# Gated cross-attention and a routed FFN on one core: the reduction of a step's first maxima is moved ahead of a layer norm's aggregation, and a third of w2's load is moved ahead of four index loads

## The reference, cut to what matters

```
x   (32, 112, 256)   ctx (32, 375, 256)   16 heads of 16
Q = LN(x) @ Wq + bq;  K = ctx @ Wk + bk;  V = ctx @ Wv + bv
attn = softmax(Q K^T / sqrt(16)) per head
x = x + tanh(g_xattn) * ((attn V) @ Wo + bo)
xf = LN(x).reshape(3584, 256)
scores = softmax(xf @ w_router.T);  w, i = top_k(scores, 2)      # 8 experts
y_e = (silu(xf @ w1[e]) * (xf @ w3[e])) @ w2[e]                  # H = 352
x = x + tanh(g_ffn) * sum_k w_k * y_{i_k}
```

## Time and profile before

| | before |
|---|---|
| median of 3 runs | 848.33 us (844.21 to 849.57) |
| the profiled execution | 848.78 us, span 847.0 us |
| TensorE | 805.1 us busy (95%) |
| VectorE, ScalarE, GpSimd | 490.0, 436.1, 525.4 us busy |
| granted TensorE clock, mean | 0.989 |
| chain that ended last | PE 70%, DVE 11%, SP's queue 8%, DMA 4% |
| DMA | 112.33 MB, 133 GB/s mean |

### The profile page before, as it was taken

One profiled execution on the slowest core, in us unless ns is written; L12 is line 12 of the kernel. 1 busy time (PEld: TensorE's weight loads), 2 busy tenths in 40 slices (PEclk: granted clock), 3 DMA queues, 4 the chain that ended last, 5 costly groups with the idle time before them and its releaser, 6 DMA issues.

```text
span 847.0 us, 22216 instructions
## 1 busy us (share of the span) xinstructions
PE 805.1 (95%) x7529; PEld 696.9 (82%) x7529; DVE 490.0 (58%) x1170; ACT 436.1 (51%) x1120; POOL 525.4 (62%) x599
## 2 busy tenths in 40 slices
PE   7889999999999999999999999888999999999995
PEld 6679899998998999999999998756777777777773
DVE  5576777877877777787777777733622222222221
ACT  3356766766676676677666666554222222222221
POOL 6554555566576667657666765436677766666652
PEclk8899999999999999999999999999999999999998
DMA  6857867776676666676657565574344444443332
GB/s 159 209 142 175 200 171 191 191 191 169 168 183 162 153 160 154 160 183 149 149 135 172 135 162 136 149 195 78 52 63 64 73 66 64 63 63 64 63 58 30
DMA packets 99733, 112.33 MB, mean 133 GB/s; under 512 B 29164, under 2 KB 81012, under 8 KB 99624
## 3 DMA queue, kind: packets, MB, share of 16 engines
q1 hardware_dynamic: 79608, 92.48, 44.4%
q0 software_dynamic: 18512, 17.60, 13.4%
q10 hardware_dynamic: 1504, 0.85, 0.5%
HBM read 35.48 MB, written 17.53 MB: 63 GB/s over the span
## 4 chain that ended last, share of the span: by engine, by line
PE 70%; DVE 11%; SPq 8%; DMA 4%; issue 3%; POOL 1%; ACT 1%; ACTq 0%; POOLq 0%; DVEq 0%
PE ps L1473 17%; PE ps L1536 10%; PE ps L1212 8%; PE ps L1195 7%; PE ps L1226 6%; PE ps L1180 6%; DVE negmax L919 5%; PE ps L1219 3%; PE ps L1329 3%; PE ps L1388 2%; PE ps L1492 2%; SPq L285 2%; DMA w_sb<-in_L_ffn_w_dram 2%; SPq L286 2%; SPq L290 2%
## 5 line engine op out<-in xcount | busy, mean ns | idle before, releaser
L919 DVE TENSOR_REDUCE negmax<-ps 112x2 f32<-112x750 f32 x256 | 239.8, 938 | 111.1 <-PE ps L1212 102.9
L620 ACT ACTIVATE probs<-ps 125x448 f32<-125x448 f32 x384 | 208.9, 545 | 83.8 <-PE ps L1180 65.1
L399 POOL DMA_DIRECT2D stack<-negmax_t x128 | 68.3, 537 | 175.3 <-ACT negmax_t L675 164.2
L1180 PE MATMUL ps<-stack 97*125 97x224 f32 x768 | 163.7, 295 | 0.6 <-ACT probs L620 0.4
L1212 PE MATMUL ps<-stack 96*112 96x376 f32 x512 | 141.3, 357 | 14.2 <-DVE negmax L919 10.3
L523 POOL DMA_INDIRECT out_dram<-y,idx x63 | 100.8, 1600 | 69.4 <-issue 32.0
L1180 PEld LDWEIGHTS ps<-stack 97*125 97x125 f32 x768 | 126.2, 187 | 7.7 <-ACT probs L620 1.2
L719 ACT ACTIVATE silu<-ps 128x352 f32<-128x352 f32 x63 | 29.3, 465 | 188.2 <-PE ps L1473 161.9
L1131 DVE TENSOR_TENSOR h<-silu,ps 128x352 f32<-128x352 f32 x63 | 32.8, 520 | 143.9 <-PE ps L1473 138.9
L1536 PE MATMUL ps<-w_sb,h_t 128*128 x378 | 92.3, 380 | 3.1 <-DMA w_sb<-in_L_ffn_w_dram 2.4
L1212 PEld LDWEIGHTS ps<-stack 96*112 96x112 f32 x512 | 71.8, 178 | 23.7 <-DVE negmax L919 14.0
(11 more groups left out here) (239 smaller groups left out, 1500.5 us busy)
## 6 DMA issues: line engine op xcount, KB each, us to landing
stack<-split SPq DMA_DIRECT2D x252, 150.0 KB
stack<-split SPq DMA_DIRECT2D x127, 94.0 KB
ctx_raw<-in_ctx_dram SPq DMA_DIRECT2D x29, 375.0 KB, 3.9
stack<-split SPq DMA_DIRECT2D x127, 56.0 KB
out_dram<-xa SPq DMA_DIRECT2D x32, 112.0 KB, 2.4
xn_scratch<-xn SPq DMA_DIRECT2D x32, 112.0 KB
xa<-in_x_dram SPq DMA_DIRECT2D x7, 448.0 KB, 4.2
w_sb<-in_L_ffn_w_dram SPq DMA_DIRECT2D x16, 176.0 KB
```

Source lines behind the costliest of these rows:

```text
L399: gp.dma_start(dst[:, :, SKP + SQ * h:SKP + SQ * h + SQ], negmax_t[4 * h:4 * h + 4, half, :].bitcast(f32)).then_inc(s_nmrow[half][c % NSLO ...
L620: act.activation(probs[:, n % NP, :], ps[0:KW, EXPB + k % 2, 0:4 * SQ], ACT.Exp).then_inc(s_exp, 1)
L919: dve.tensor_reduce(negmax[:, half, :, p4], ps[0:SQ, m1:m2 + 1, 0:SK], axis=AX.X, op=ALU.max, negate=True).then_inc(s_max, 1)
L1180: last = pe.matmul(ps[0:KW, EXPB + k % 2, QW * m:QW * m + QW], stack[:, place_of(b), p, KW * ch:KW * ch + KW], stack[:, place_of(b), p, SK ...
```

## The change

Two edits. VectorE's reduction of the first pair of maxima of a step (t = 0, for batches 1 to 31; batch 0 keeps its place) is no longer taken in slot 0 behind `xn`, but in slot 11 of the step before. The copy of the logits moves up too, so that slot 11 now reads: copy of the logits, first maxima of batch i+2, aggregation, halving. In SyncE's list, the load of w2's first 128 rows (1024 KB) stands directly behind the eight loads of w3's second half, in front of the first four index loads; the other two parts stay where they were, behind these index loads and two stores.

```diff
@@ SyncE, step(i == LAST - 2)
                         sp.dma_start(w3_hi[:, e, :], w3[e, P:2 * P, :]).then_inc(s_w13, 16)
+                    sp.dma_start(w2_sb[:, 0, :, :], w2[:, 0:P, :].rearrange("e p d -> p e d")).then_inc(s_w2, 16)
                     for t in range(4):
                         load_idx(t)
@@ SyncE, step(i == LAST - 1)
-                    for c in range(FC):
+                    for c in range(1, FC):
                         n = min(P, F - P * c)
@@ VectorE
+            def maximum(c, t):
+                half, p4 = t // 4, t % 4
+                dve.wait_ge(s_max_ps, 8 * c + t + 1)
+                if p4 == 0:
+                    wait(dve, s_nm_ps, 2 * c + half - 1)
+                m1, m2 = max_banks(c, t)
+                dve.tensor_reduce(negmax[:, half, :, p4], ps[0:SQ, m1:m2 + 1, 0:SK], axis=AX.X, op=ALU.max, negate=True).then_inc(s_max, 1)
@@ VectorE, step(i)
-                    if k in MAX_IN and c is not None:
-                        t = MAX_IN.index(k)
...
+                    if k in MAX_IN and c is not None and (k > 0 or c == 0):
+                        maximum(c, MAX_IN.index(k))
...
+                    if k == 11 and i == GB * SNAP + 7:
+                        dve.wait_ge(s_tot, 1)
+                        link(dve.tensor_copy(n_rest[:, :], ps[0:1, BB_, CT:CT + NE]))
+                    if k == 11 and r is not None:
+                        dve.wait_ge(s_lg_ps, r + 1)
+                        dve.tensor_copy(lg[:, r // GB % 2, r % GB, :], ps[0:SQ, BB_, LG:LG + NE]).then_inc(s_lg, 1)
+                    if k == 11 and i >= -1 and live(i + 2) is not None:
+                        maximum(i + 2, 0)
                     if k == 11 and e is not None:
                         dve.wait_ge(s_st2, e + 1)
                         wait(dve, s_xn2, e - 1)
                         link(dve.bn_aggr(mv2[:, e % 2, :], st2[:, :]))
                         dve.tensor_scalar(half2[:, :], mv2[:, e % 2, 1:2], LN_EPS, -0.5, ALU.add, ALU.mult).then_inc(s_half2, 1)
-                    if k == 11 and i == GB * SNAP + 7:
-                        dve.wait_ge(s_tot, 1)
-                        link(dve.tensor_copy(n_rest[:, :], ps[0:1, BB_, CT:CT + NE]))
...
-                    if k == 11 and r is not None:
-                        dve.wait_ge(s_lg_ps, r + 1)
-                        dve.tensor_copy(lg[:, r // GB % 2, r % GB, :], ps[0:SQ, BB_, LG:LG + NE]).then_inc(s_lg, 1)
```

## The result

| | before | after |
|---|---|---|
| median of the runs | 847.68 us (844.21 to 849.57, 4 runs) | 856.1 us (855.56 to 857.66, 4 runs) |
| ratio, 95% interval | | 1.0101 [1.0064, 1.0138] |
| the profiled execution, its span | 848.78, 847.0 | 855.63, 853.8 |
| granted TensorE clock, mean | 0.989 | 0.978 |

The changed kernel is 1.0% slower: +8.6 us (+5.4 to +11.7), where I forecast -4.9 against the profiled execution. The time lies outside my range and nearest to the third rival (852.1).

The account below looks back on a forecast made before the run. TensorE was taken as the bound, held up by VectorE at step boundaries and by w2 at the change of phase. 848.78 (profiled execution) - 5.7 (VectorE's edit) + 0.8 (load edit) = 843.9 us, range 840.0 to 848.5.

Parts of the forecast that it names:

- the third rival: Change of phase: gathers of tiles 0 and 1 report only when w2's rest is in, 569.5; 852.1 us, chance 0.06.
- Edit 1, boundary: Step boundaries: TensorE's gap from exponentials to second pair shrinks from 0.52 to 0.30 at 18; 6.9 us gained over all boundaries.
- The sign that I named for it: TensorE's list of waits: the wait for reductions of maxima falls from 10.3 us by some 5.
- What moves back costs nothing as I read it: Step boundaries: delayed aggregation, halving, logarithm, row DMAs and normed batch have enough cover, so they cost 0.
- Edit 1, late keys: Four boundaries with late stacked keys lose again the gain of the boundary just ahead: 1.2 us given back.
- Rival 2: Step boundaries: stacked keys set the pace and two thirds of the gain are given back; 847.7 us, chance 0.12.
- rival 4: Step boundaries: VectorE waits in order, ScalarE behind it, half of the 5.7 us lost in ScalarE's queue; 846.8, chance 0.08.
- Edit 2, the index: Change of phase: tile 0's index lands behind w2's first part, 3.0 us later; gather at 557.1 instead of 554.12.
- I take 4.2, between the two: Change of phase: tile 0's gather to transposes takes 4.2 us, between 3.28 and 5.1; transposes at 561.3, not 557.40.
- Edit 2, w2's wait: Change of phase: TensorE's 2.41 us wait for w2 vanishes, yet w2's matmuls start at 573.4 instead of 572.61, 0.8 lost.

Follow-up runs that it names:

- e3: e1 with the router's slot sum put back in front of the moved first reduction of maxima: 842.18 us, ratio 0.995 to the kernel before.
- e5: e3 with the slots' product, sum and cast moved from slot 1 behind the third reduction in slot 2: 841.13 us, ratio 0.9934 to the kernel before.
- e1: The changed kernel without the load edit, all of w2 loaded where it was: 845.32 us, ratio 0.9978 to the kernel before.
- e6: The changed kernel with w2's other two parts held until the first two gathers have landed: 847.75 us, ratio 1.001 to the kernel before.
- e7: The changed kernel with 20 and 60 unread transposes filling TensorE's waits in step 31: 853.07 us, ratio 1.0073 to the kernel before.
- e4: The kernel before, with w2's first part directly behind the four index loads: 849.54 us, ratio 1.0029 to the kernel before.

## Why the prediction was wrong

**Edit 1, boundary: right in mechanism and size.** Gap 0.29, forecast 0.30; the step 0.28 shorter, forecast 0.22. The sign that I named for it was wrong: TensorE's wait for the reductions should have fallen by some 5 us and fell by 0.5. At a regular boundary the second pair's row shows no wait at all, so closing its gap takes nothing off that list. What is on it: at the second pairs 2.2 us before and 0.7 after, at the fourth pairs, which stand behind the casts, 1.1 before and 2.2 after, and the rest little changed.

**Edit 1, "What moves back costs nothing as I read it": this step failed.** I followed aggregation, halving, the row DMAs and the normed batch, and not what else stands behind the moved reduction at only some boundaries. The slot sum does, at six, with TensorE waiting for it in its next slot. By the steps' lengths the six lost 2.1 us where they should have gained 1.7. The five steps with the cast lost 1.1 where they should have gained 1.4. Together that would be 6.3 us; undoing it took 3.7 and 1.8 us off these steps in the profiles of e3 and e5, and moved the times by 3.7 (-1.9 in e1, -4.2 in e3, -5.6 in e5, this one with an interval of -7.9 to -3.2). I had checked TensorE's gap at all 31 boundaries, and VectorE's queue at one.

**Edit 1, late keys: right.** Three boundaries waited 2.2 us for stacked keys, forecast four at about what they were the earlier trace rows. Rival 2 fell. So did rival 4: no new wait for ScalarE shows among the largest. Rival 4 had it right that edit 1 would not bring its gain, but VectorE's queue took it away, not ScalarE's.

**Edit 2, the index: right in mechanism, too small, and its number hit by luck.** The gather went at 557.07, and I forecast 557.1. But that forecast was in before's time, and the phase began 1.7 us earlier. From step 31's values to the gather it is 10.8 us instead of 6.1: +4.7 where I had +3.0. I priced the load at its bytes over 346 GB/s.

**Edit 2, "I take 4.2, between the two": this failed, and the largest part of the miss is here.** The change of phase came out 9.85 us longer, forecast 0.8. Of the 9.05 between, the index has 1.7, this step 4.3, and the way from rows to w2, below, 3.05. From gather to rows it was 8.5, and e6 shows what did it: with w2's rest issued behind the rows it is 3.0, with the index as late. The rows of a gather issued 1.5 us behind 1.8 MB of loads were usable at 565.58, when the loads' last packets were in (565.3). That is what rival 3 forecast, to which I gave 0.06, and by its own mark: tile 0's transposes came 6.0 us behind my 561.3, counted in before's time. Its 852.1 was still 4.0 too low, since it kept the whole 5.7 of edit 1. I had dismissed the rule behind it by one row: tile 1's rows at 560.65 while w2 was under way until 572.5. That row doesn't speak against it. Tile 1's gather was issued at 555.50 to 556.49, w2's three parts from 555.78 to 559.95: so at most the first part was ahead of it. Issue order, not "under way", was what to compare. The packets bear it out: before, tile 1's rows moved from 558.45 to 560.04, while w2 went on to 572.0.

Why they wait is less clear than that they do. The Trainium skill says (DMA: Bandwidth & Descriptors, section "Queues, rings and completion order") that a completion's increment lands only after every earlier write of the same DMA engine, across its queues. The order of events agrees with it, but it would make finished rows report late, and the packets show rows that moved late: 5.2 of the 8.5 us passed before the gather's first packet, where it is 1.8 with the loads held back (e6). From its last packet to the transposes it is 1.28 us, against 0.47 in e6, so some 0.8 us at most are left for that rule.

**Edit 2, w2's wait: gone, and paid for again.** From tile 0's rows to w2's matmuls TensorE needed 15.21 - 2.41 = 12.80 us before and 15.15 after, the first 8.3 of them at half clock; my forecast had 12.1 (561.3 to 573.4). I had no term for the clock. It fell after a wait of 2.15 us for rows of negated maxima, issued at 547.06 and 547.5, beside w2's first part; before, they kept TensorE 0.17 us. e7 puts the clock's price near 2.4 us, weakly: with only 3.4 us of that stretch at half clock it still needed 14.39.

**In sum.** Edit 1 -1.9 (-4.1 to +0.4) instead of -5.7; edit 2 +7.5 (+4.9 to +10.2) instead of +0.8.

**Open.** The cast's 0.98 us is put down to GpSimd by their common ends, and by the 0.17 us that it takes where GpSimd stands still (e5); no run changed GpSimd alone. What decides in which runs the clock falls in the change of phase is open as well: it fell in e1 at 553.9, behind waits of 0.60, 0.42, 1.04, 0.22 and 0.25 us, and not in e5 behind 0.60, 0.42, 0.62, 0.21, 0.25, 0.76 and 1.41. Whether e4's edit on top of e5 would bring something was not tried; e4's times give no reason, its shorter change of phase gives some.

## What to carry to other kernels

When an instruction moves ahead in an engine's queue, list what it now delays in every variant of the step, the rare ones too, and for each who waits for it next. When a bulk load moves ahead, count every small transfer issued behind it, those of other queues too, and price it at the load's full landing, twice where an index and its gather follow each other. Compare a transfer with the order of issue before you read it as proof that it can pass another.

## What the runs showed of the hardware

- A gather on GpSimd's queue, issued 1.5 us after two loads (1.8 MB) on SyncE's queue, was usable after 8.5 us, and its first packet moved 5.2 us after the issue. Where the first part of w2 (1 MB) was issued within 0.8 us of the gather, before or behind it, the rows were usable after 4.3 us (e4), 5.1 (before, tile 1) and 6.3 (e5, tile 1); with no load of w2 issued in the 9 us ahead of it, after 3.0 (e6).
- An index load of 1 KB, issued 1.6 us behind a load of 1 MB on the same queue, released its gather 8.0 us after its issue, and 3.6 us in the kernel before, without that load.
- VectorE's cast of 112x8 numbers took 0.98 to 1.09 us in four steps in which it ended with a GpSimd addition, 0.27 to 0.28 where it ended with GpSimd's norm (before), and 0.17 while GpSimd stood still. The Trainium skill (SBUF — State Buffer, section "SBUF: two separate sides") says that some VectorE operations and GpSimd's share a port pair and the loser waits for the whole instruction. The common ends agree with that; two casts of the changed kernel do not, since they took 0.40 (from 176.92) and 0.27 (from 440.06) and ended while GpSimd's norm ran on.
- The granted clock stood at 0.50 for 20 us after a stand of 2.15 us with shorter ones around it, and came back while TensorE was busy.
